# One SBUF region for projection, scoring and message rows; six message groups gathered ahead, in a graph-attention kernel

## The reference, cut to what matters

```python
x = x + gat(layernorm(x))     # 2500 x 512, 40000 edges (src, dst), 8 heads of 64
x = x + ffn(layernorm(x))     # 8 experts, each token weighted by its best two

def gat(x):
    h_e, h_r = x @ W_e, x @ W_r                       # per head
    diff = h_r[dst] - h_r[src]
    score = s_src[src] + s_dst[dst] + diff . a_dif + |diff| . a_abs + (h_r[src] * h_r[dst]) . a_prd
    alpha = leaky_relu(score, 0.2)
    ex = exp(alpha - segment_max(alpha, src)[src])
    att = ex / (segment_sum(ex, src)[src] + 1e-16)
    return segment_sum(att * h_e[dst], src)           # the "messages"
```

## Time and profile before

| what | value |
|---|---|
| median of three runs | 1518.27 us |
| the profiled execution's own time | 1517.85 us |
| its span | 1516.1 us |
| PE, DVE, ACT, POOL busy | 85%, 80%, 67%, 58% |
| granted TensorE clock, mean | 0.93 of full speed |

### The profile page before, as it was taken

One profiled execution on the slowest core, in us unless ns is written; L12 is line 12 of the kernel. 1 busy time (PEld: TensorE's weight loads), 2 busy tenths in 40 slices (PEclk: granted clock), 3 DMA queues, 4 the chain that ended last, 5 costly groups with the idle time before them and its releaser, 6 DMA issues. The chain is left out here.

```text
span 1516.1 us, 25712 instructions
## 1 busy us (share of the span) xinstructions
PE 1281.4 (85%) x6763; PEld 747.1 (49%) x6764; DVE 1207.1 (80%) x2409; ACT 1013.3 (67%) x2459; POOL 876.0 (58%) x953
## 2 busy tenths in 40 slices
PE   6999939999999999999539999999998056999940
PEld 2555525555555555555325555555554035777730
DVE  8998778999999999999748999999999953212217
ACT  5555417888989899898547898888886033555510
POOL 2100017777777777776647777777775803665520
PEclk9999969999999999999759999999999576999975
DMA  8111127888887887888569877777775093343439
GB/s 234 42 63 71 49 94 222 229 232 235 224 231 235 231 230 231 236 227 240 169 214 371 248 225 230 227 234 248 227 225 145 15 329 135 132 131 131 136 119 345
DMA packets 127712, 295.35 MB, mean 195 GB/s; under 512 B 29090, under 2 KB 45206, under 8 KB 127466
## 3 DMA queue, kind: packets, MB, share of 16 engines
q0 software_dynamic: 62880, 207.55, 46.6%
q1 hardware_dynamic: 62634, 85.29, 16.8%
q10 hardware_dynamic: 2080, 1.05, 0.3%
HBM read 247.91 MB, written 45.92 MB: 194 GB/s over the span
## 5 line engine op out<-in xcount | busy, mean ns | idle before, releaser
L1166 PE MATMUL m_ps<-msg,hot 128*128 128x512 f32 x672 | 369.5, 643 | 29.1 <-ACT msg L1108 28.9
L1085 POOL DMA_INDIRECT g<-he_d,target x288 | 293.4, 1019 | 94.1 <-issue 72.2
L927 PE MATMUL gs_ps<-room,hot_t 128*128 x1008 | 274.1, 381 | 10.3 <-DVE hot_t L787 8.7
L1002 ACT ACTIVATE uv<-ab,raw_a 128x512 f32<-128x512 f32 x336 | 273.7, 815 | 11.2
L768 POOL DMA_INDIRECT x_sb<-table_d,target x220 | 231.2, 1051 | 72.4 <-issue 51.2
L1000 ACT ACTIVATE ab<-d_ps 128x512 f32<-128x512 f32 x336 | 196.1, 584 | 74.9 <-PE d_ps L940 73.9
L798 DVE TENSOR_TENSOR uv<-uv,ab 128x512 f32<-128x512 f32 x336 | 229.3, 682 | 3.0 <-ACT uv L1002 2.8
L1136 DVE TENSOR_TENSOR room<-m_ps,room 128x512 f32 x336 | 229.8, 684 | 1.5 <-PE m_ps L1166 0.4
L1168 PEld LDWEIGHTS den_ps<-room,hot 128*128 128x128 f32 x672 | 129.2, 192 | 163.9 <-issue 163.9
L1129 DVE TENSOR_TENSOR msg<-g,room 128x384 f32<-128x384 f32 x336 | 184.4, 549 | 27.9 <-DMA g<-he_d,target 23.2
L1108 ACT ACTIVATE msg<-g,room 128x64 f32<-128x64 f32 x672 | 168.9, 334 | 56.3 <-DMA g<-he_d,target 52.9
(11 more groups left out here) (304 smaller groups left out, 2035.8 us busy)
## 6 DMA issues: line engine op xcount, KB each, us to landing
early_d<-early_rows SPq DMA_DIRECT2D x48, 256.0 KB, 3.1
g<-early_d SPq DMA_DIRECT2D x12, 1024.0 KB, 7.6
x_sb<-local_d SPq DMA_DIRECT2D x84, 128.0 KB, 4.2
w_sb<-in_L_ffn_W_dram SPq DMA_DIRECT2D x16, 512.0 KB, 8.0
pair_rows<-pairs_d SPq DMA_DIRECT2D x8, 1024.0 KB, 13.0
table_d<-row POOLq DMA_DIRECT2D x20, 260.0 KB, 2.6
he_d<-he SPq DMA_DIRECT2D x20, 256.0 KB, 2.0
xn_d<-xn SPq DMA_DIRECT2D x10, 512.0 KB, 4.9
```

What stands on the lines that cost most here:

```text
L927: pe.matmul(gs_ps[:, use(n, t) % 3, :], h, hrs[:, bass.ds(blk, 1), piece, :].rearrange("p a f -> p (a f)"), start=(piece == 0), stop=(piec ...
L1002: act.activation(uv[:, j, c, :], ab[:, j, c, :], ACT.Identity, bias=raw[:, 0, c:c + 1], scale=raw[:, 1, c:c + 1]).then_inc(ur, 1)
L1085: pool.indirect_dma_start(g[:, r, t, :, :, :].rearrange("p c h d -> p (c h d)"), None, he_d, bass.IndirectOffsetOnAxis(ap=k["target"][:, q ...
L1166: pe.matmul(m_ps[:, i % BK, :], hot[:, r, t, :], msg[:, r, t, :, :, :].rearrange("p c h d -> p (c h d)"), start=True, stop=True).then_inc( ...
```

## The change

One new tensor, `rows` (8,192 + 4,160 columns of f32), takes the place of several. In the first block it holds the weights, a scratch and two rings; in the scoring it holds `ab`, `uv` and the two far homes of the gather ring; after the scoring its first part is the six homes of the message ring, which until now was allocated only in the third block. So message rows can be gathered to their homes before the block of the messages begins. The small scratches `hm` and `run`, which lay in `ab`, move to `extra`.

With that, three things change in the order of work:

- Six message groups (0 to 5, 24 tiles) are gathered straight to their homes by POOL in the scoring block, after the accumulator is cleared. POOL first waits until the last transposes, the last `extras` and the last score sums are done, because those read the region. The message block's POOL list starts with group 6, and so with a wait.
- The early groups are now six, 9, 22, 35, 48, 61 and 74, so 24 tiles, all gathered among the scoring gathers as before; the 24 gathers and stores that stood behind the scoring are gone. SP loads six times 1 MB in the message block.
- SP's load of x (4.9 MB) follows the load of group 9 and thus the wait for group 3.

```diff
-EARLY_EVERY, EARLY_ROOM = 7, 3
-EARLY = -(-G // EARLY_EVERY)
-BESIDE = GT * EARLY // 2
+AHEAD, EARLY_ROOM = 6, 3
+EARLY_GROUPS = tuple(range(9, G, 13))
+ROWS_ROOM = 2 * CH * LC * 2 + (RING - FLAT) * GT * TW
 ...
-        w_e = s.sb("w_e", [P, CH, F])
-        w_r = s.sb("w_r", [P, CH, F])
+        part_of = lambda n: k["rows"][:, n * CH * F:(n + 1) * CH * F]
+        w_e = part_of(0).rearrange("p (c f) -> p c f", c=CH)
+        w_r = part_of(1).rearrange("p (c f) -> p c f", c=CH)
 ...
-        gd_more = s.sb("gd_more", [P, RING - FLAT, GT, TW])
+        half = 2 * CH * LC
+        ab, uv = (k["rows"][:, n * half:(n + 1) * half].rearrange("p (r c j) -> p r c j", r=2, c=CH) for n in range(2))
+        gd_more = k["rows"][:, 2 * half:].rearrange("p (r t w) -> p r t w", t=GT, w=TW)
 ...
             @block.sync          # score_edges
-                for e in range(BESIDE, GT * EARLY):
-                    keep_early(e)
 ...
             @block.gpsimd        # score_edges
-                for e in range(BESIDE, BESIDE + GT * EARLY // 4):
-                    gather_early(e)
                 pool.wait_ge(gathered, GT * G)
                 pool.memset(k["acc"], 0.0).then_inc(cleared, 1)
-                for e in range(BESIDE + GT * EARLY // 4, GT * EARLY):
-                    gather_early(e)
+                pool.wait_ge(dturned, CH * G)
+                pool.wait_ge(extras, G)
+                pool.wait_ge(red, G)
+                for n in range(AHEAD):
+                    q = message_tile(n)
+                    for t in range(GT):
+                        pool.indirect_dma_start(k["msg_rows"][:, n, t * F:(t + 1) * F], None, he_d,
+                                                bass.IndirectOffsetOnAxis(ap=k["target"][:, q + t:q + t + 1], axis=0)).then_inc(k["msg_rows_in"][n], 16)
                 pool.wait_ge(cleared, 1)
 ...
             @block.gpsimd        # sum_messages
-                for n in range(G):
+                for n in range(AHEAD, G):
                     if is_early(n):
                         continue
                     r, q = n % ROWS, first_tile(n)
-                    if n >= ROWS:
-                        pool.wait_ge(made, GT * (n - ROWS + 1))
-                        pool.wait_ge(made_act, GT * (n - ROWS + 1))
+                    pool.wait_ge(made, GT * (n - ROWS + 1))
+                    pool.wait_ge(made_act, GT * (n - ROWS + 1))
```

More of the change, by code:

```diff
@@ L65, in early_turn @@
     past = [m for m in range(EARLY_ROOM, n) if m % 10 in (0, 4, 8)]
-    now = n >= EARLY_ROOM and n % 10 in (0, 4, 8) and len(past) < BESIDE
+    now = n >= EARLY_ROOM and n % 10 in (0, 4, 8) and len(past) < GT * len(EARLY_GROUPS)
     return len(past) if now else None
@@ L146, in project_and_sort @@
         xn = s.sb("xn", [P, 2, F])
-        xt = s.sb("xt", [P, XT, CH, P])
-        row = s.sb("row", [P, XB, TW])
+        xt = part_of(3).rearrange("p (r c n) -> p r c n", r=XT, c=CH)
+        row = k["rows"][:, 4 * CH * F:4 * CH * F + XB * TW].rearrange("p (r w) -> p r w", r=XB)
         he = s.sb("he", [P, 2, F])
@@ L698, in score_edges @@
         extra = s.sb("extra", [P, 2, GT, CH, 16, 2])
+        spare = extra[0:1, :, :, :, :, :].rearrange("p r t c s h -> p (r t c s h)")
+        hm = spare[:, 0:4 * P].rearrange("p (n c h s) -> p n c h s", n=4, c=CH, h=2)
+        run = spare[:, 4 * P:6 * P].rearrange("p (n c h s) -> p n c h s", n=2, c=CH, h=2)
         al = s.sb("al", [P, L])
@@ L745, in _ @@
                         keep_early(e)
-                for e in range(BESIDE, GT * EARLY):
-                    keep_early(e)
                 for j in range(EARLY_ROOM):
-                    sp.wait_ge(early_out[j], 16 * len(range(j, GT * EARLY, EARLY_ROOM)))
+                    sp.wait_ge(early_out[j], 16 * len(range(j, GT * len(EARLY_GROUPS), EARLY_ROOM)))
             @block.gpsimd
             def _(pool):
[L753 to L758, removed]
                 for n in range(SOON, G):
@@ L1027, in sum_messages @@
 def sum_messages(nc, k, sem, x, he_d, early_d):
-    RING, ROWS, BK = 4, 6, 6
+    RING, ROWS, BK = 4, AHEAD, 6
     HV = 3
@@ L1043, in sum_messages @@
         made, made_act, offs = sem("m_made"), sem("m_made_act"), sem("m_off")
-        got = [sem(f"m_rows_in{r}") for r in range(ROWS)]
+        got = k["msg_rows_in"]
         xback, clear, den_done = sem("x_back"), sem("x_tail_then_den_clear"), sem("den_done")
@@ L1062, in _ @@
             def _(sp):
-                for n in range(0, G, EARLY_EVERY):
-                    r, lo = n % ROWS, n // EARLY_EVERY * GT * P
-                    if n >= ROWS:
-                        sp.wait_ge(made, GT * (n - ROWS + 1))
-                        sp.wait_ge(made_act, GT * (n - ROWS + 1))
+                for i, n in enumerate(EARLY_GROUPS):
+                    r, lo = n % ROWS, i * GT * P
+                    sp.wait_ge(made, GT * (n - ROWS + 1))
+                    sp.wait_ge(made_act, GT * (n - ROWS + 1))
                     sp.dma_start(g[:, r, :, :, :, :].rearrange("p t c h d -> p t (c h d)"),
                                  early_d[lo:lo + GT * P, :].rearrange("(t p) f -> p t f", p=P)).then_inc(loaded, 16)
-                    if n == EARLY_EVERY:
+                    if i == 0:
                         sp.dma_start(x_sb[:, 0:NB - 1, :], x[0:(NB - 1) * P, :].rearrange("(b p) f -> p b f", p=P)).then_inc(xback, 16)
@@ L1723, in kernel_body @@
             )
+            k["rows"] = e.sb("rows", [P, ROWS_ROOM])
+            k["msg_rows"] = k["rows"][:, 0:AHEAD * GT * F].rearrange("p (r w) -> p r w", r=AHEAD)
+            k["msg_rows_in"] = [sem(f"m_rows_in{r}") for r in range(AHEAD)]
             with ExitStack() as scoring:
```

21 lines of the change are left out of this document (10 added, 11 removed).

## The result

The changed kernel takes 1527.34 us (median of 4 runs, 1525.46 to 1528.15), the one before 1517.8 us; the ratio is 1.0059, with a 95% interval of 1.0046 to 1.0071. It is slower, by some 9 us, as forecast in sign, but 4.3 us more than the forecast and 0.3 us above its range (1517.5 to 1527.0 us). The profiled execution took 1527.8 us with a span of 1526.1 us, 10.0 us more than the one before.

The account below looks back on a forecast made before the run. POOL's chain of 288 gathers was taken to bound the message block. 1.5 + 2.5 + 0.7 = +4.7 us on 1517.85 us gave 1522.6, with the median 0.4 higher 1523.0 us; range 1517.5 to 1527.0 us.

Parts of the forecast that it names:

- That POOL's gathers set the message stage: Message block: one long chain of 288 POOL gathers, 1.322 us each, sets its length, not PE's matmuls.
- The meeting: Scoring's end to message block's start: release at 779.1 us, POOL's first gather at 783.2 instead of 781.70 us, +1.5 us.
- the meeting does not wait for landings: Rival at the scoring's end: release at 774.6 us, soon after POOL's last issue; sum +0.2, 1518.5 us; chance 12%.
- The second wait: Message block, group 10: POOL arrives at 20.0 us, before DVE has multiplied group 4 at 22.5 us; +2.5 us.
- The rate: Message block: the first 24 gathers slow from 1.295 to 1.325 us each as DVE has rows at once; +0.7 us.
- the holds: Message block: gathers lengthened by DVE instructions (L1129) stay about one in four, 20 us in sum, 2 us either way.
- the rule weighed against the rows: Skill page's inference that DVE's SBUF reads do not hold descriptor writing; the prediction sided with rows showing gathers held beside softmax.
- After the last gather everything is as before: Message block's end: the 10.3 us from last gather to last additions stay, and nothing is added behind.

## Why the prediction was right and where it failed

*That POOL's gathers set the message stage* held. Every run moved its end with POOL's first gather and the number of gathers: five groups ahead began 10.1 us sooner with 4 gathers more (5.3 us) and its last gather was 4.15 us sooner.

*The meeting, +1.5 us: 4.3 us measured.* The chain was right (last gather ahead, POOL's drain, ACT's first group, POOL's first gather), with most pieces too short. The gathers ahead ended at 775.65 instead of 774.0 us, since the last score sums came 1.7 us later than before (743.20 us) and the first gather 0.8 us behind them; in the stretch itself 24 took 31.6 us where I had 32.4. In the eight other executions with this order of scoring the sums ended from 1.5 us sooner to 1.7 us later than here, so part of the 1.7 us is spread. ACT's start came 5.61 us after the last gather where I had taken 5.1 (781.26 against 779.1 with the later end). ACT's first group took 4.0 us, as worked out (4.1), to 785.24 us, but POOL's gather started 0.77 us behind it, which I had at nothing: all of POOL's waits in the earlier trace rows were over before it asked, so they did not show what an awaited release costs. (At groups 7 and 10 it was only 0.26 us: see the last section.)

*The rival "the meeting does not wait for landings"* gave a release at 774.6 us, right behind the last issue; ACT began at 781.26 us, and leaving the drain out shows that POOL's drain is what takes the time. But my own reading, that POOL drains only when its gathers have landed, is not shown, and the traces speak against it: the same drain took 8.8 us with no group ahead, when the last gather lay 32 us back. The length taken over from the earlier trace rows fitted (5.3 us to the drain's end, 5.6 us to ACT's start); that the reason given for it did not matter is luck.

*The second wait, +2.5 us: 2.16 us* at group 10 (2.46 less the usual 0.30), by the lead of POOL over DVE as computed, and 0.54 us at group 7 that I had not seen.

*The rate, +0.7 us: about -2.1 us.* The first 24 gathers did become slower (the offset to before grows from 4.31 to 7.55 us over them, 2.7 us of it the two waits), but then it shrank to 4.96 us by the last. What the gathers took beyond 0.95 us each came to 17.7 us against 19.8. In the other three executions of the changed order it was 18.3 to 19.0 us, in two others of the order before 18.9 and 20.2 us, so over several executions the gain is nearer 1 us. From 812 us on DVE waits for rows more (28.9 us, against 17.1), and a waiting DVE holds no gather, which would fit; no run tests it. I had taken the holds to stay as they were and given 2 us for them either way.

Together these made +5.0 us against +4.7 us forecast, and that closeness is luck: the meeting was 2.8 us too short and the rate 2.8 us too long. On the rule weighed against the rows, the trace stays with the rows: 24 gathers beside the softmax took 31.6 us where 30.0 us would do without holds, and seven of them were longer than 0.96 us.

*The step that failed* is "After the last gather everything is as before". It was so up to the last additions (11.45 us behind the start of the last gather, 11.28 before), but the stage does not end there. POOL's drain at the stage's end cost nothing before, 1.70 us beside 2.9 us of DVE, and I priced it at nothing without naming that cover; it became 8.57 us, +5.3 us. I had looked at a drain at the scoring's end, where the change moves gathers up to it, and not at the other one, which the diff does not touch. Leaving this drain out gave 5.2 us back. Why it became long is open. No row of the kernel before shows a long one at that place; the end of the expert stage, where POOL's drain took 7.73 us in both kernels, would have been a warning of the size.

## What to carry to other kernels

Gathers that an engine issues ahead of a stage's end can be paid for in its closing instruction there, and in the one a stage later, so price the whole way from its last issue to the next stage's first instruction, at both ends of the stage, and name what covers it. Before moving gathers up to a boundary, ask whether the boundary must drain: the same order lost 9.5 us with the scoring's drain and won 4 us without it. A change that removes one of two equal holds (SP's stores) shows nothing until the other (POOL's drain) is removed as well.

## What the runs showed of the hardware

- POOL's drain can be long after gathers, and not by waiting for them to land: it ended 4.7 to 5.5 us behind the last gather at the ends of the first two stages, where gathers stood right before it, 8.55 us behind it where it was put behind the last of the message stage, 8.57 us behind POOL's last instruction at that stage's end although the last gather had ended 40 us before that instruction, and it took 8.8 us with no group ahead, 32 us after the last gather. No drain took over 9.1 us by itself, with 4 to 766 gathers and scatters since the one before. Done once, the next is short (0.08 us). It is work that can be placed where POOL is idle.
- Without the drain a stage begins while POOL still gathers for the one before: ACT at 770.97 us, POOL's last gather of the scoring until 773.58 us.
- What a real wait for a semaphore costs a gather of POOL came in two sizes. It started 0.26 us behind the release where the gather itself carried the wait that ended last (791.55 against 791.29 us and 804.35 against 804.09 us, both behind DVE), and 0.74 to 0.8 us where that wait stood in an instruction of its own ahead of the gather (786.01 against 785.24 us behind ACT, 744.01 against 743.24 us behind the score sums). The semaphores' times in the traces of the other runs show the same two sizes. Where the release is past, only the 0.30 us between any two gathers remain.
- Two holds can end a stage together: in the kernel before, SP's last store and POOL's drain were 0.4 us apart, and leaving the drain out gained nothing.
